# Graph attention on one NeuronCore: four heads' scores issued together, one product and one tanh per unit over four PSUM banks

## The chip, the cores and the metric

The kernel runs on one core of a Trainium2 chip. Its engines are TensorE (PE, and PEld for its weight loads), VectorE (DVE), ScalarE (ACT), GpSimd (POOL) and the queue of SyncE (SP), which only issues transfers here. The metric is the time of the program on the device in microseconds (us), as the median of the runs; lower is better.

## The reference

Sixteen graphs of 512 nodes with 256 features pass through four residual layers: a graph convolution, a mixture of 8 experts, a graph attention, and a mixture of 64 experts with a shared expert. The change lies in the third layer and in the pieces of the fourth that are computed alongside it:

```python
Xp = jnp.einsum('bnd,hdk->bhnk', X, Wp) + bp[None, :, None, :]
Xc = jnp.einsum('bhnk,hjk->bhnj', Xp, C)
attn = jnp.tanh(A[:, None] * jnp.einsum('bhnj,bhmj->bhnm', Xc, Xp))
Xh = jnp.einsum('bhnm,bhmk->bhnk', attn, Xp)
out = jnp.moveaxis(Xh, 1, 2).reshape(X.shape[0], X.shape[1], -1)
return jax.nn.relu(out)
# and of the fourth layer, for every token:
shared = jax.nn.silu(xf @ sw1) * (xf @ sw3) @ sw2
logits = xf @ gate_w.T          # scores, the best two experts, places in the experts' buffers
```

There are 8 heads of 32 features. X is the layer norm of the running activations x, and A is the weighted adjacency of each graph.

## The kernel before

The program is a chain of phases: the graph convolution, the first experts, the attention phase (`attention_phase`), and the second experts with the final sums. Every engine has its own program, written out by hand, and semaphores order them. There is no scheduler: an instruction waits behind all that stand ahead of it on its engine.

The attention phase loops over 16 graphs. The 8 heads of a graph form 2 groups of 4 (`HG = 4`), and the 512 nodes form 4 tiles of 128, so a graph has 8 units (`UNITS`), unit u being group u // 4 and tile u % 4. For each unit:

- `scores` (L1408, PE): for each of the 4 heads a product of 32 rows of weights with 512 columns, in three terms (high by high, high by low, low by high), into one PSUM bank per head of `p_s`. Head i lies on partitions 32i to 32i+31. The unit is done in two halves c, with two heads each, so a half has 6 matmuls.
- `products` (L1914, DVE): `att` = `p_s` times the adjacency, one instruction per half (128x1024 elements).
- `tanhs` (L1712, ACT): tanh in place on `att`, one instruction per half.
- `values` (L1421, PE): four heads' matmuls of `att` with 32 columns of weights each, accumulated over the 4 tiles of a group into `p_o`.

`att` has two buffers (`u % 2`), so the product of unit u waits for the values of unit u-2. `p_s` takes four of the eight PSUM banks, `p_o` one, and the three banks of `p_w` serve all side work. In the loop of PE a half's scores for unit u+1 are issued as soon as the product of the same half of unit u is done, while DVE multiplies the other half:

```python
for c in range(2):
    pe.wait_ge(prod_ready, 2 * (UNITS * b + u) + c + 1)
    ... scores(b, h, u + 1, c)        # in the last unit: the next graph's unit 0
    if c == 0:
        side_a(u)
        values(b, h, u - 1)
    else:
        side_b(u)
```

Side work is placed by hand after units. On PE: `turn` (L1428, transposes of the normalised x for the next graph and for the fourth layer), `turn_back` (L1434), `wide` (L1440, 512 columns by 256 features: two for the projection of the next graph, four for the shared expert of the graph before), `project_c` (L154 to L156), `logits` (L1452), `down` (L1459), `count_before` (L937, L939), and `keep_busy` (L1465), a matmul whose result nobody reads. The four shared `wide` and the two `down` exist only for the first 8 graphs (`OWN`); later graphs have `keep_busy` in their place and have their shared expert done in the next phase. I call graphs 2 to 8, which have all of it, full graphs, and graphs 10 to 15 late graphs. On ACT: `apply1` and `apply3` (layer norm applied, L1674 and L1683), the evacuations of `p_w`, `exps` (L1703), `silus` (L1707). On DVE: `stats1` and `stats3` (L175, L180), `add_attention` (L1824), `add_shared` (L1834), `split_projection` and `split_c` (L160), `gate_shared` (L1829), and the router's steps `scores_of`, `best_of`, `members_of`, `places_of`, `own_places_of`, `rows_of` (L1839 to L1907). On POOL: `weigh_moe0` and `add_moe0` (the first experts' results for the graph after next), `scale1` and `scale3`, and `scatter` of rows into the second experts' buffers. SP loads the adjacency of the next graph.

Of the kernel before, what the change touches and what calls it, by code (L numbers as in the profile page):

```python
# [23 lines left out]
P = 128  # L24
# [1137 lines left out]
def attention_phase(nc, a, m, sb):  # L1162
# [3 lines left out]
    with ExitStack() as ctx:  # L1166
# [54 lines left out]
        of = lambda f, par: 0 if f == 0 else 1 + par  # L1221

# [30 lines left out]
        def _(sp):  # L1253
# [22 lines left out]
            def graph(q, h, first, last):  # L1276
# [7 lines left out]
                if not last:  # L1284
                    if not is_at(b, 0):
                        sp.wait_ge(prod_ready, 2 * UNITS * b + T)
                    load_adj(b + 1, 1 - h)
# [9 lines left out]
        def _(pool):  # L1297
# [71 lines left out]
            def graph(q, h, first, last):  # L1369
                b = 2 * q + h  # L1370
                more = not (isinstance(b, int) and b + 2 >= B)
                if is_at(b, 0):
                    scale1(1)
                if more:
                    weigh_moe0(b + 2)
                if not is_at(b, 0):
                    scale3(b - 1)
                if more:
                    add_moe0(b + 2)
                if not (isinstance(b, int) and b < 2):  # L1380
                    scatter(q - 1, h, b - 2, 0)
                    scatter(q - 1, h, b - 2, 1)
                if more:
                    scale1(b + 2)

# [14 lines left out]
        def _(pe):  # L1400
            def scores(b, par, u, c):
# [3 lines left out]
                for n, (left, right) in enumerate(((xpth, xcth), (xpth, xctl), (xptl, xcth))):  # L1405
                    for i in (2 * c, 2 * c + 1):
# [4 lines left out]
            def values(b, par, u):  # L1411

                f, t = u // T, u % T
                pe.wait_ge(att_ready, 2 * (UNITS * b + u) + 2)
# [22 lines left out]
            def wide(w, f, src, bank, done, last_of=False):  # L1437

                for k in range(KD):
                    mm = pe.matmul(p_s[:, bank, :] if last_of else p_w[:, bank, :], w[:, k, f * P:(f + 1) * P], src[:, k, :],  # L1440
                                   start=(k == 0), stop=(k == KD - 1))
                mm.then_inc(done, 1)
# [24 lines left out]
            def project_first():  # L1467

                pe.wait_ge(xn_ready, 1)
                turn(xn, 0, 1, tr_done)  # L1470
                turn(xn, 1, 2, tr_done)
# [3 lines left out]
                wide(wp, 0, xt, 0, xpt_done)  # L1475
                wide(wp, 1, xt, 1, xpt_done)
                pe.wait_ge(xpt_ready, 1)
                turn_back(xpf[:, 0], 2, xp_done)
                pe.wait_ge(xp_ready, 1)
                pe.wait_ge(xpt_lo, 1)  # L1480
                pe.wait_ge(cd_split, 2)
                project_c(0, 0, 2)
                pe.wait_ge(xpt_ready, 2)
                pe.wait_ge(xpt_lo, 2)
                project_c(0, 1, 0)
                pe.wait_ge(xct_lo, 1)
                turn_back(xpf[:, 1], 2, xp_done)
                scores(0, 0, 0, 0)
                scores(0, 0, 0, 1)

            def graph(q, h, first, last):
# [4 lines left out]
                z, w = h, 1 - h  # L1496

                def side_a(u):
                    if u == 0 and late:
                        pe.wait_ge(member_ready, b - 1)  # L1500
# [4 lines left out]
                        count_before(pe, m, count, member, count_done)  # L1505
                    if u == 1 and post:
                        pe.wait_ge(ot_ready, GRP * b)
                        if late:
                            pe.wait_ge(r2_step, R2 * (b - 2) + 2)
                        else:  # L1510
                            pe.wait_ge(xp_ready, GRP * b + 2)
                        turn_back(ot[:, 1], 2, back_done)
                    if u == 2 and not last:
                        pe.wait_ge(xn_ready, b + 2)
                        if going_down:
                            pe.wait_ge(x4_ready, TB * (b - 2) + 1)
                        else:
                            pe.wait_ge(xct_lo, GRP * b + GRP)
                        turn(xn, 0, z, tr_done)
                        if post:  # L1520
                            pe.wait_ge(x3_ready, GRP * b)
                        else:
                            pe.wait_ge(xp_ready, GRP)
                        turn(xn, 1, 2, tr_done)
                    if u == 3 and post:
                        pe.wait_ge(xn3_ready, b)
                        if last:
                            pe.wait_ge(xct_lo, GRP * b + GRP)
                        turn(xn3[:, 1 - h], 0, z, tr3_done)
                        turn(xn3[:, 1 - h], 1, 2, tr3_done)  # L1530
                    if u == 4 and not last:
                        pe.wait_ge(xpt_ready, GRP * (b + 1) + 1)
                        if post:
                            pe.wait_ge(xt3_ready, KD * b)
                        turn_back(xpf[:, 0], 2, xp_done)
                    if u == 5:
                        pe.wait_ge(ot_ready, GRP * b + 1)
                        if not last:
                            pe.wait_ge(xpt_ready, GRP * (b + 1) + 2)
                        turn_back(ot[:, 0], z, back_done)  # L1540
                    if u == 6 and going_up:
                        pe.wait_ge(x3_ready, GRP * b + 1)
                        wide(ws3, 0, xt3, z, up_done)
                    if u == 7 and going_up:
                        pe.wait_ge(xp_ready, GRP * (b + 1) + 2)
                        wide(ws1, 1, xt3, 2, up_done)
                    if u == 6 and post and not going_up:
                        pe.wait_ge(x3_ready, GRP * b + 1)
                        keep_busy(z)
                    if u == 7 and post and not going_up:  # L1550
                        keep_busy(z)

                def side_b(u):
                    if u == 0 and going_down:
                        pe.wait_ge(hs_ready, KHS * (b - 1))
                        pe.wait_ge(xct_lo, GRP * b + GRP)
                        down(0, z)
                    if u == 1 and going_down:
                        down(1, w)
                    if u == 2 and not last:  # L1560
                        pe.wait_ge(xt_ready, KD * (b + 2))
                        if going_down:
                            pe.wait_ge(x4_ready, TB * (b - 1))
                        elif post:
                            pe.wait_ge(x3_ready, GRP * (b - 1) + 1)
                        else:
                            pe.wait_ge(xpt_ready, GRP)
                        wide(wp, 0, xt, w, xpt_done)
                    if u == 3 and not last:
                        if post:  # L1570
                            pe.wait_ge(xt3_ready, KD * (b - 1) + 1)
                        wide(wp, 1, xt, z, xpt_done)
                    if u == 4 and post:
                        pe.wait_ge(xt3_ready, KD * b)
                        if last:
                            pe.wait_ge(x3_ready, GRP * (b - 1) + 1)
                        logits(xt3, w)
                    if u == 4 and not last:
                        pe.wait_ge(xp_ready, GRP * (b + 1) + 1)
                        pe.wait_ge(xpt_lo, GRP * (b + 1) + 1)  # L1580
                        project_c(1 - h, 0, 2)
                    if u == 5 and going_up:
# [799 lines left out]
```

## Time and profile before

| | |
|---|---|
| median of 3 runs | 2228.31 us (2223.23 to 2232.1) |
| span of the profiled execution | 2229.1 us |
| PE busy over the span | 2052.3 us, 92% |
| DVE busy | 1538.2 us, 69% |
| ACT busy | 1246.9 us, 56% |
| POOL busy | 1062.8 us, 48% |
| attention phase, first to last product | 1024.5 to about 1741 us |

The profiled execution's own time is the span; it lies inside the range of the three runs. Busy shares are means over phases with different limits, so the attention phase has to be read by itself. The granted clock (PEclk) is the clock that TensorE was given: 1.00 stands for 2.4 GHz and 0.50 for 1.2 GHz.

### The profile page before, as it was taken

The page shows a single profiled execution, that of the slowest core. Times are in us where ns is not written, and L with a number is a line of the kernel's source. Part 1 is how long each engine was busy: PE and PEld are TensorE (multiplying, and loading weights), DVE is VectorE, ACT ScalarE, POOL GpSimd, SP SyncE. Part 2 cuts the span into 40 slices and gives each one's busy share as a digit, 9 for nine tenths or more (in the row PEclk, how much of TensorE's full clock was granted, in tenths as well). Part 3 has the DMA queues.
Part 4 walks back from the last instruction along what each step waited for, and adds up shares of the span by engine and source line. Part 5 has one row for each costly group of instructions (what it writes and reads, how often), then busy time and mean ns, then how long its engine had stood idle before and what let it go on. Part 6 is the DMA issues. An engine that isn't in the chain of part 4 may idle for free. (4 is left out here: it accounts for less than half of the span.)

```text
span 2229.1 us, 38475 instructions
## 1 busy us (share of the span) xinstructions
PE 2052.3 (92%) x12194; PEld 1499.7 (67%) x12194; DVE 1538.2 (69%) x3332; ACT 1246.9 (56%) x1870; POOL 1062.8 (48%) x1266
## 2 busy tenths in 40 slices
PE   7999999956999999967999999999999789999986
PEld 6988888845888888853454544444444478888853
DVE  6777777744666666654687778887876557767759
ACT  4444444414666666645766766675666257767630
POOL 3355555552333333326345565464642447777740
PEclk9999999977999999987999999998998899999998
DMA  7344445125555555643122211223221055556559
GB/s 288 146 170 172 171 171 181 39 82 172 167 184 175 176 183 172 179 152 132 57 95 83 98 62 62 77 82 103 74 67 32 6 181 182 187 167 191 187 204 350
DMA packets 138148, 315.42 MB, mean 142 GB/s; under 512 B 36990, under 2 KB 67808, under 8 KB 133952
## 3 DMA queue, kind: packets, MB, share of 16 engines
q1 hardware_dynamic: 106560, 271.77, 36.3%
q0 software_dynamic: 31488, 42.39, 5.5%
q8 instruction: 54, 0.88, 0.2%
q14 instruction: 46, 0.38, 0.1%
HBM read 206.67 MB, written 151.56 MB: 161 GB/s over the span
## 5 line engine op out<-in xcount | busy, mean ns | idle before, releaser
L1712 ACT ACTIVATE c_att<-c_att 128x1024 f32<-128x1024 f32 x256 | 270.0, 1057 | 210.5 <-DVE c_att L1914 208.3
L1914 DVE TENSOR_TENSOR c_att<-c_p_s,adj 128x1024 f32<-128x1024 f32 x256 | 301.1, 1216 | 86.5 <-PE c_p_o L1421 74.4
L2241 POOL DMA_INDIRECT moe_y<-d_y,d_goal x256 | 257.0, 1004 | 115.9 <-ACT d_y L2206 51.5
L995 POOL DMA_INDIRECT moe_y<-b_y,b_goal x144 | 155.4, 1079 | 327.8 <-DVE b_y L1047 293.9
L1408 PEld LDWEIGHTS c_p_s<-c_xcth,c_xpth 32*128 32x128 f32 x512 | 48.0, 185 | 208.3 <-issue 121.2
L154 PE MATMUL b_p_y<-b_w2h,b_hh 128*128 128x256 f32 x576 | 169.2, 294 | 7.4 <-DVE b_hl L160 4.0
L476 POOL DMA_INDIRECT moe_in<-a_xn,a_rows x128 | 141.5, 1106 | 57.6 <-issue 29.2
L160 DVE TENSOR_TENSOR b_hl<-b_ht,b_hh 128x512 fp32r<-128x512 f32 (+1 forms) x160 | 101.5, 638 | 88.8 <-ACT b_ht L1153 88.8
L155 PE MATMUL b_p_y<-b_w2l,b_hh 128*128 128x256 f32 x576 | 160.7, 279 | 0.0
L156 PE MATMUL b_p_y<-b_w2h,b_hl 128*128 128x256 f32 x576 | 160.6, 279 | 0.0
L1364 POOL DMA_INDIRECT moe_in<-c_xn,c_rows x128 | 130.6, 1020 | 53.8 <-issue 39.4
L1408 PE MATMUL c_p_s<-c_xcth,c_xpth 32*128 32x512 f32 x512 | 130.0, 505 | 27.0 <-DVE c_att L1914 26.2
L1421 PE MATMUL c_p_o<-c_att,c_xp 128*32 128x512 f32 x1024 | 143.4, 633 | 0.0
L160 DVE TENSOR_TENSOR d_xl<-d_p_tr,d_xh 128x1024 fp32r<-128x1024 f32 x64 | 78.4, 1225 | 75.7 <-ACT d_xh L2196 75.7
L154 PE MATMUL b_p_h<-b_xh,b_w1h 128*128 128x512 f32 (+1 forms) x320 | 120.7, 377 | 7.1 <-DVE b_w1l L160 4.7
L1330 POOL TENSOR_SCALAR c_nm<-c_mv 128x4 f32<-128x4 f32 x32 | 8.1, 254 | 245.4 <-DVE c_mv L180 245.2
L154 PEld LDWEIGHTS b_p_y<-b_w2h,b_hh 128*128 128x128 f32 x576 | 108.0, 188 | 18.5 <-DVE b_hl L160 15.9
L155 PE MATMUL b_p_h<-b_xl,b_w1h 128*128 128x512 f32 (+1 forms) x320 | 119.9, 375 | 0.0
L156 PE MATMUL b_p_h<-b_xh,b_w1l 128*128 128x512 f32 (+1 forms) x320 | 119.8, 374 | 0.0
L1148 ACT ACTIVATE b_w2h<-b_w 128x1024 fp32r<-128x1024 f32 x40 | 42.5, 1063 | 136.9 <-PE b_p_y L156 122.1
L1152 ACT ACTIVATE b_hh<-b_p_h,b_b 128x512 fp32r<-128x512 f32 (+1 forms) x160 | 103.8, 649 | 23.3 <-PE b_p_h L156 10.9
L1313 POOL TENSOR_SCALAR c_g<-c_g,c_ggate 128x256 f32<-128x256 f32 x120 | 110.8, 941 | 6.1 <-DMA c_g<-moe_y 3.1
(273 smaller groups left out, 6147.4 us busy)
## 6 DMA issues: line engine op xcount, KB each, us to landing
b_w<-in_moe_w SPq DMA_DIRECT2D x80, 512.0 KB, 4.3
moe_in<-b_zeros SPq DMA_DIRECT2D x65, 520.0 KB, 10.8
d_xin<-moe_in SPq DMA_DIRECT2D x64, 520.0 KB, 3.5
adj<-in_adj SPq DMA_DIRECT2D x32, 1024.0 KB, 5.6
b_xin<-moe_in SPq DMA_DIRECT2D x32, 520.0 KB, 5.9
c_g<-moe_y SPq DMA_DIRECT2D x32, 512.0 KB
moe_y<-c_zeros SPq DMA_DIRECT2D x32, 512.0 KB
d_w<-in_moe_w SPq DMA_DIRECT2D x64, 256.0 KB
```

Source lines behind the costliest of these rows:

```text
L154: pe.matmul(out, lh, rh, start=start, stop=False)
L155: pe.matmul(out, lh, rl, start=False, stop=False)
L156: return pe.matmul(out, ll, rh, start=False, stop=stop)
L160: return dve.tensor_tensor(low, whole, high.bitcast(F32), ALU.subtract)
L476: pool.indirect_dma_start(out=m["moe0_in"], out_offset=bass.IndirectOffsetOnAxis(ap=rows[:, h, k, t:t + 1], axis=0), in_=xn2[:, h, t, :], ...
L995: pool.indirect_dma_start(out=m["moe0_y"], out_offset=bass.IndirectOffsetOnAxis(ap=goal[:, h, t:t + 1], axis=0), in_=y[:, h, t, :], in_off ...
L1364: pool.indirect_dma_start(out=m["moe1_in"], out_offset=bass.IndirectOffsetOnAxis(ap=rows[:, par, k, t:t + 1], axis=0), in_=xn3[:, par, t, ...
L1408: mm = pe.matmul(p_s[:, i, :], left[r, s, tok], right[r, f, :], start=(n == 0), stop=(n == 2))
L1421: mm = pe.matmul(p_o[DH * i:DH * i + DH, :], xp[:, par, t, col:col + DH], att[:, u % 2, i, :], start=(t == 0), stop=(t == T - 1))
L1712: act.activation(part, part, ACT.Tanh).then_inc(att_ready, 1)
L1914: dve.tensor_tensor(att[:, u % 2, 2 * c:2 * c + 2, :], p_s[:, 2 * c:2 * c + 2, :], adj[:, h, u % T, :].unsqueeze(1).broadcast_to([P, 2, N] ...
L2241: pool.indirect_dma_start(out=m["moe1_y"], out_offset=bass.IndirectOffsetOnAxis(ap=goal[:, h, t:t + 1], axis=0), in_=y[:, h, t, :], in_off ...
```

## The change

Every unit is handled whole. `scores(par, u)` issues 12 matmuls, the four heads in turn within each of the three terms. One DVE instruction makes the product over all four banks (128x2048 elements) and one ACT instruction the tanh. PE now issues the scores of unit u at the head of iteration u, after the product of unit u-1, where it had issued those of unit u+1 after a half of the product of unit u. The banks of `p_w` get fixed names, and nearly all side work moves by a unit or so: the second `project_c` and the second `turn_back` of the projection go into units 0 and 1 of the graph that uses them, `logits` from unit 4 to 5, one shared `wide` into the next graph's unit 0, `apply1` from the first unit to the last of the graph before, and two `wide` are cut in two between neighbouring units. On POOL `add_moe0` comes before `scale3`, and `scale1` before the second `scatter`. The number of matmuls, of side instructions and of `keep_busy` per graph stays the same.

```diff
-            def scores(b, par, u, c):
+            def scores(par, u):
                 for n, (left, right) in enumerate(((xpth, xcth), (xpth, xctl), (xptl, xcth))):
-                    for i in (2 * c, 2 * c + 1):
+                    for i in range(HG):
                         mm = pe.matmul(p_s[:, i, :], left[r, s, tok], right[r, f, :], start=(n == 0), stop=(n == 2))
                 mm.then_inc(s_done, 1)
...
                 for u in range(UNITS):
-                    for c in range(2):
-                        pe.wait_ge(prod_ready, 2 * (UNITS * b + u) + c + 1)
-                        if u + 1 < UNITS:
-                            if u + 1 == T and c == 0:
-                                pe.wait_ge(xct_lo, GRP * b + 2)
-                            scores(b, h, u + 1, c)
-                        elif not last:
-                            scores(b + 1, 1 - h, 0, c)
-                        if c == 0:
-                            side_a(u)
-                            if u > 0:
-                                values(b, h, u - 1)
-                            elif post:
-                                values(b - 1, 1 - h, UNITS - 1)
-                        else:
-                            side_b(u)
+                    if post or u > 0:
+                        pe.wait_ge(prod_ready, UNITS * b + u)
+                    if u % T == 0:
+                        pe.wait_ge(xct_lo, GRP * b + u // T + 1)
+                    scores(h, u)
+                    side_a(u)
+                    if u > 0:
+                        values(b, h, u - 1)
+                    elif post:
+                        values(b - 1, 1 - h, UNITS - 1)
+                    side_b(u)
...
-            def tanhs(b, u, c):
-                act.wait_ge(prod_ready, 2 * (UNITS * b + u) + c + 1)
-                part = att[:, u % 2, 2 * c:2 * c + 2, :]
-                act.activation(part, part, ACT.Tanh).then_inc(att_ready, 1)
+            def tanhs(b, u):
+                act.wait_ge(prod_ready, UNITS * b + u + 1)
+                act.activation(att[:, u % 2], att[:, u % 2], ACT.Tanh).then_inc(att_ready, 1)
...
-            def products(b, h, u, c):
+            def products(b, h, u):
                 n = UNITS * b + u
-                if c == 0 and not (isinstance(n, int) and n < 2):
+                if n > 1:
                     dve.wait_ge(av_done, n - 1)
-                dve.wait_ge(s_done, 2 * n + c + 1)
-                dve.tensor_tensor(att[:, u % 2, 2 * c:2 * c + 2, :], p_s[:, 2 * c:2 * c + 2, :],
-                                  adj[:, h, u % T, :].unsqueeze(1).broadcast_to([P, 2, N]), ALU.mult)\
+                dve.wait_ge(s_done, n + 1)
+                dve.tensor_tensor(att[:, u % 2], p_s[:], adj[:, h, u % T, :].unsqueeze(1).broadcast_to([P, HG, N]),
+                                  ALU.mult)\
```

PE's side work by unit after the change (`side_b`, after the values, but for one piece of unit 4 that stands ahead of them as `side_a`), in a full graph: 0: `wide`, `count_before`, `project_c`; 1: `turn_back`, `down`, `turn_back`; 2: two `turn`, `down`; 3: one and a half `wide`; 4: half a `wide` (`side_a`), two `turn`; 5: two `turn_back`, `logits`; 6: `project_c`, one and a half `wide`; 7: one and a half `wide`. In a late graph the pieces of the shared expert fall away and `keep_busy` stands in units 0, 1, 6 and twice in 7.

DVE's side work after the product of the unit, in a full graph: 0: `gate_shared`, `places_of`; 1: `split_c`, `add_attention`, `stats3`, `add_shared`; 2: `own_places_of`, `add_shared`; 3: `rows_of`; 4: `split_projection`, `stats1`; 5: `add_attention`, `split_projection`; 6: `scores_of`, `best_of`; 7: `split_c`, `gate_shared`, `members_of`.

ACT's after the tanh: 0: `evac_c`; 1: `evac_tokens`; 2: two `evac_turned`, `apply3`; 3: `evac_projection`; 4: two `evac_turned`, `evac_projection`; 5: `exps`, `evac_tokens`; 6: `evac_c`, `silus`; 7: `silus`, `apply1`.

## Rows read from the trace of the kernel before

**Rows 1.** The page, its head.

```profile
span 2229.1 us, 38475 instructions
```

**Rows 2.** Windows: stretch, length, PE, PEld, DVE, ACT, POOL busy, PEclk, DMA, GB/s.

```profile
1024.00:1744.00 720.00, 691.54 (x3887) 324.36 (x3879) 549.08 (x1116) 468.08 (x637) 359.88 (x512) 0.96 0.23 77
...
1187.80:1234.60 46.80, 46.04 (x261) 22.55 (x259) 37.01 (x76) 31.66 (x44) 26.39 (x38) 1.00 0.26 86
...
1559.00:1601.20 42.20, 40.02 (x239) 18.39 (x237) 34.47 (x72) 27.74 (x40) 25.51 (x36) 1.00 0.29 92
```

**Rows 3.** Line 1703 on ACT, once per graph: first and last start in three stretches.

```profile
L1703 ACT ACT_TABLE_LOAD  x9: 1283/1283/1283, 1093.2 to 1467.3; - x9
...
L1703 ACT ACTIVATE c_sg<-c_p_w x2: 385/386/386, 1510.0 to 1558.6; 128x256 f32<-128x256 f32 x2
...
L1703 ACT ACTIVATE c_sg<-c_p_w x3: 384/385/386, 1558.6 to 1643.0; 128x256 f32<-128x256 f32 x3
```

**Rows 4.** Timeline of PE in a full graph: start, time, line, instructions, idle before.

```profile
1205.90 0.49 PE L1408 MATMUL c_p_s<-c_xcth,c_xpth 32*128 32x512 f32 x2
1206.24 0.39 PE L1408 MATMUL c_p_s<-c_xctl,c_xpth 32*128 32x512 f32 x2
1206.47 0.39 PE L1408 MATMUL c_p_s<-c_xcth,c_xptl 32*128 32x512 f32 x2
...
1207.31 1.07 PE L1421 MATMUL c_p_o<-c_att,c_xp 128*32 128x512 f32 x8
1208.31 0.50 PE L1408 MATMUL c_p_s<-c_xcth,c_xpth 32*128 32x512 f32 x2
...
1209.19 1.99 PE L1459 MATMUL c_p_w<-c_ws,c_sh 128*128 128x256 f32 x8
1211.12 0.50 PE L1408 MATMUL c_p_s<-c_xcth,c_xpth 32*128 32x512 f32 x2
...
1217.54 1.09 PE L1428 MATMUL c_p_w<-consts,c_xn 128*128 128x128 f32 x8
...
1232.14 2.00 PE L1452 MATMUL c_p_w<-c_wg,c_xt 128*128 128x64 f32 x16
...
1234.82 0.50 PE L1408 MATMUL c_p_s<-c_xcth,c_xpth 32*128 32x512 f32 x2
...
1238.21 1.98 PE L1440 MATMUL c_p_w<-c_xt,c_ws 128*128 128x512 f32 x4
1240.03 0.60 PE L1434 MATMUL c_p_w<-consts,c_xpf 128*128 128x128 f32 x4
1240.56 0.50 PE L1408 MATMUL c_p_s<-c_xcth,c_xpth 32*128 32x512 f32 x2
```

**Rows 5.** Timeline of PE in a late graph, same columns.

```profile
1564.51 0.50 PE L1408 MATMUL c_p_s<-c_xcth,c_xpth 32*128 32x512 f32 x2 [1.18 <-DVE c_att L1914]
...
1565.40 1.13 PE L1465 MATMUL c_p_w<-c_xt,consts 128*128 128x512 f32 x2
1566.45 1.07 PE L1421 MATMUL c_p_o<-c_att,c_xp 128*32 128x512 f32 x8
```

**Rows 6.** Timeline of DVE in a full graph, same columns.

```profile
1213.55 1.40 DVE L175 BATCH_NORM_STATS2 c_st<-x 128x6 f32<-128x256 f32 x4
...
1215.39 2.32 DVE L1914 TENSOR_TENSOR c_att<-c_p_s,adj 128x1024 f32<-128x1024 f32 x2
...
1218.23 0.16 DVE L1890 TENSOR_SCALAR c_fits<-c_ownpos 128x8 f32<-128x8 f32 x1
...
1221.79 2.34 DVE L1914 TENSOR_TENSOR c_att<-c_p_s,adj 128x1024 f32<-128x1024 f32 x2
```

**Rows 7.** Groups by line: busy us, mean ns of one, then idle before.

```profile
L1712 ACT ACTIVATE c_att<-c_att 128x1024 f32<-128x1024 f32 x256 | 270.0, 1057 | 210.5 <-DVE c_att L1914 208.3
...
L1693 ACT ACTIVATE c_xcth<-c_p_w 128x512 fp32r<-128x512 f32 x32 | 18.8, 587 | 3.9 <-PE c_p_w L156 3.9
```

**Rows 8.** Windows, columns as in rows 2, a stretch at the lower clock.

```profile
1516.00:1530.00 14.00, 13.93 (x43) 4.61 (x43) 7.39 (x22) 5.08 (x6) 11.31 (x15) 0.51 0.02 5
```

More of the change, by code:

```diff
@@ L1495, in graph, with side_b @@
                 going_up, going_down = post and b - 1 < OWN, late and b - 2 < OWN
[L1496 removed]
                 def side_a(u):
[L1499 to L1500 removed]
+                    if u == 4 and not last:
+                        wide(wp, 1, xt, LEFT, xpt_done, only=(1,))
+                def side_b(u):
+                    if u == 0:
+                        if going_down:
+                            wide(ws3, 1, xt3, RIGHT, up_done)
+                        elif late:
+                            keep_busy(RIGHT)
+                        if late:
+                            pe.wait_ge(member_ready, b - 1)
+                            if going_down:
+                                pe.wait_ge(hs_ready, KHS * (b - 2) + 1)
+                            else:
+                                pe.wait_ge(xp_ready, GRP * b + 1)
+                            count_before(pe, m, count, member, count_done)
+                        pe.wait_ge(xpt_ready, GRP * b + 2)
+                        pe.wait_ge(xpt_lo, GRP * b + 2)
@@ L1513, in side_a @@
-                    if u == 2 and not last:
-                        pe.wait_ge(xn_ready, b + 2)
+                        elif late:
+                            pe.wait_ge(sg_ready, b - 1)
+                        project_c(h, 1, LEFT)
+                    if u == 1:
+                        if post:
+                            pe.wait_ge(ot_ready, GRP * b)
+                            if late:
+                                pe.wait_ge(r2_step, R2 * (b - 2) + 2)
+                            else:
+                                pe.wait_ge(xp_ready, GRP * b + 1)
+                            turn_back(ot[:, 1], COUNT, back_done)
+                        if going_down:
+                            pe.wait_ge(hs_ready, KHS * (b - 2) + 2)
+                            down(0, RIGHT)
+                        elif late:
+                            keep_busy(RIGHT)
+                        pe.wait_ge(xct_lo, GRP * b + 2)
+                        turn_back(xpf[:, 1], LEFT, xp_done)
@@ L1544, in side_a @@
[L1544 to L1563, printed above, removed]
-                        elif post:
[L1565 to L1582, printed above, removed]
-                        pe.wait_ge(sg_ready, b)
-                        wide(ws1, 0, xt3, w, up_done)
-                    if u == 5 and not last:
-                        pe.wait_ge(xct_lo, GRP * (b + 1) + 1)
-                        turn_back(xpf[:, 1], 2, xp_done)
-                    if u == 6 and not last:
-                        pe.wait_ge(xpt_lo, GRP * (b + 1) + 2)
```

292 lines of the change are left out of this document (148 added, 144 removed).

## The prediction

> **What bounds the kernel now.** I read the page's head first, for the span, 2229.1 us [rows 1]; the median of the runs, 2228.3, is the same within their spread, so I sum against 2228. Then a window over the attention phase, which alone is touched: 720 us, PE busy 691.5, DVE 549.1, ACT 468.1 [rows 2]. Then one graph by itself. The step that happens once per graph comes every (1467.3 - 1093.2)/8 = 46.8 us in the graphs that carry the shared expert, and every (1643.0 - 1558.6)/2 = 42.2 us in late ones [rows 3]. In a full graph PE is busy 46.04 of 46.8 us, DVE 37.0, ACT 31.7; in a late one PE 40.0 of 42.2, DVE 34.5 [rows 2]. The reader is to see that PE is the bound: it idles 0.8 us in a full graph and 2.2 us in a late one, the latter in two pieces such as the 1.18 us wait for a product [rows 5].
>
> What is PE busy with? I read starts against starts, since matmul ends are modelled and overlap. A half of the scores is three rounds of two matmuls, starting at 0, 0.34 and 0.57 us, the round being 0.23 us; the values after it start 1.00 us before the next scores; those take 0.88 us until the next work starts [rows 4]. So a unit costs 2 x 0.88 (scores) + 1.00 (values) = 2.76 us, and a graph 22.1. The side work, likewise: `down` 1.93, a pair of `turn` 1.09 by its modelled end (I take 1.03), `logits` with `project_c` 2.68, `wide` 1.82 to 1.98 (I take 1.9), `turn_back` 0.53 to 0.6 [rows 4]; `count_before` lies between the end of a half's scores and the values, 1207.31 - 1205.90 - 0.88 = 0.5; `keep_busy` 1.05 [rows 5]. With 6 `wide`, 2 `down`, 2 pairs of `turn`, 4 `turn_back`, 2 `project_c` (0.88 each) and the rest this is about 23.8 us in a full graph. 22.1 + 23.8 + 0.8 idle = 46.7, against 46.8 found. In a late graph it is 17.5; 22.1 + 17.5 + 2.2 = 41.8 against 42.2.
>
> **The scores.** The two matmuls of a round read and fill different groups of 32 rows of the array and take 0.23 us together, what 512 columns take one after the other at 2.4 GHz (213 ns): they run side by side [rows 4]. The trace has no round of four. Bounds: four side by side cost what two do, a unit's scores falling from 1.76 to 0.88; or only two go at once, and nothing is saved. The values show four matmul groups of 32 columns side by side, 8 instructions in 1.00 us [rows 4], which is near the first bound, so I take it: 8 x 0.88 = 7.0 us of PE per graph.
>
> The Trainium skill has a rule against the full gain ("TensorE: Matmul & The Clock Gate", Measured speedup vs the span model): four row tiles of 32 at 512 columns gained 3.07 times, not 4. By it a round would be 4/3.07 x 0.23 = 0.30 us, an estimate, and 3 x 128 x 0.07 = 27 us of the gain would be lost, giving 2185. The pairs here show no such loss; no row here shows four.
>
> **What is lost with the halves.** Before, PE wrote one half while DVE read the other, so a product never waited for its scores. Now the chain of a unit is serial. From the start S of its scores: last result and hand-over at 1.04 (0.96 and 0.08); product 2.27 (a pair now takes 2.32 to 2.34 [rows 6], one instruction saves a start; bounds 2.2 and 2.35); tanh at S + 3.38, 2.0 long (1057 ns for 1024 elements and 587 for 512 [rows 7] extend to 1997; bounds 2.0 and 2.11); values at S + 5.44 at the earliest. Next scores can't start before S + 3.37. PE's own order would bring it to these values at S + 1.88 + s + 0.88, s being the side work of the unit. So values wait when s < 2.7, and the wait is longer when DVE reached the product late. Behind the waiting values stand all of `side_b` and the next scores.
>
> **A full graph by hand.** PE's side work after the change, by unit 0 to 7: 3.3, 3.1, 3.0, 2.85, 2.0, 3.0, 3.7, 2.85, all cost as above. DVE's: 1.25, 3.65, 2.0, 3.56 (`rows_of`, 1218.23 to 1221.79), 2.45, 1.2, 2.4, 2.95; `stats3` is 1.84 of it, 1213.55 to 1215.39 [rows 6]. After product 1 DVE has 3.65 us of side work, one us more than its gap, so product 2 is 1.0 late and its values hold PE 0.7. After product 3 `rows_of` makes product 4 start 1.8 after its scores; PE, whose unit 4 is short, waits 0.3 for it and 1.2 for its values. In unit 5 `logits` wait until ACT has evacuated the projection, some 0.1. Elsewhere the values are ready by under 0.3. ACT's heaviest spot, two evacuations and `apply3` after tanh 2, delays tanh 3 by 0.9 but PE comes later still. PE then needs 8 x 1.88 + 23.8 = 38.8 of work plus 2.3 of waits, 41.1 us. Gain 5.7.
>
> **A late graph by hand.** Side work of PE by unit: 2.4, 2.2, 1.0, 2.85, 2.0, 3.0, 1.9, 2.1, all but two below 2.7. Waits: 0.3 (values 0), 1.2 for product 2 and 1.2 for its values, 0.7 in unit 5, 0.2 before `logits`, 0.8 for values 6, 0.3 more spread. 15.0 + 17.5 + 4.7 = 37.2. Gain 5.0, cut to 4.9.
>
> **POOL and SP.** POOL is busy 26.4 of 46.8 us [rows 2] and would be 26 of 41. `rows_of` ends after some 22 us of the graph, so the two scatters and `scale1` end near 34; the next weighing and adding then end some 6 us into the next graph, and `scale3` waits for `stats3` at 12. Nothing late reaches ACT: `apply3` comes at 17. Moving `scale1` ahead of the second scatter serves `apply1` at the end of the graph; if it were late by all of a scatter (5 us), `turn` in unit 2 has 9 us left. The adjacency is loaded after two units, as before, 6 units ahead of use. Cost nothing.
>
> **Sum.** Graphs 2 to 8: 7 x 5.7 = 40. Graphs 1 and 9, with half of the shared work: 5 each, 10. Graphs 10 to 15: 6 x 4.9 = 29. Graph 0, with little side work, 3. Together 82.
>
> **The clock.** Over the phase the granted clock averages 0.96, which is 58 us at 1.2 GHz and 29 us of PE's time lost [rows 2]. One such stretch, 14 us at 0.51 [rows 8], lies in a late graph, the kind that has PE waits of over 1 us, and the once-per-graph step took 1558.6 - 1510.0 = 48.6 us across it instead of 42.2 [rows 3]: 6.4 more. I put half of the 29 us to the twelve waits of 1 us or more in the six late graphs (the split is an estimate): 1.2 us a wait. The change puts one such wait into each of nine graphs that had none and perhaps one more into the first: 10 x 1.2 = 12. Bounds: -29 (the low stretches vanish) and +74 (each graph gets one like that, 16 x 6.4, less the 29 there are). I take +12.
>
> 2228 - 82 + 12 = **2158**.
>
> **Rivals.** (a) *Four row groups don't run together.* PE saves nothing, while the serial chain puts some 1 us of waits for late products into each graph: 2228 + 16 + 12 = 2256, slower. For: no row shows four. Against: pairs at no cost, and values four wide. It decides from a round of 0.23 + 70/(3 x 128) = 0.41 us on. 0.06. (b) *The hand-over binds.* Each unit costs DVE its work plus the 1.04 of scores, which side work doesn't cover: 37.0 - 1.3 + 8.3 = 44.0 in a full graph, 34.5 - 1.3 + 8.3 = 41.5 in a late one; gains 9 x 2.8 + 6 x 0.7 = 29, with the clock's 12 a time of 2211. Against: side work stands just after the product, so while PE scores. A middle between this and my schedule is 2185. 0.16 for 2185 to 2215. (c) *The clock falls in every graph*: 2228 - 82 + 74 = 2220, no change; from 2 x 70 = 140 us more at 1.2 GHz on it is a loss. 0.09, a third each of slightly faster, same, slower. (d) *The waits don't come*: PE saves all, 16 x 7.0 = 112, less the clock's 0 to 12, 2115 to 2130. 0.12. My case: 0.57.
>
> **Numbers.** Mine alone spans 2130 to 2185: one us more or less of waits a graph is 16, a clock of -10 to +15 more. The range for 8 in 10 goes into (d) and (b): 2115 to 2206. Less than 0.5%, 11 us, can't be told from no change. Faster: 0.57 + 0.12 + 0.16 + 0.03 = 0.88; same 0.04 (c and the edge of b); slower 0.08 (a and the rest of c).
>
> **What would show it.** Rounds of x4 scores 0.23 us apart, the next work 0.88 us after their start; a once-per-graph step every 41 us, then every 37; PE busy near 39 of 41; PE waits of about 1 us for `att` from ACT in unit 5 and for the product in late graphs; product 2.2 to 2.3 us, tanh 2.0; DVE waiting for `c_p_s` where it hardly does now. It is wrong if rounds are 0.4 us, if the step still comes every 44 us with DVE never idle, or if PEclk over the phase falls below 0.90.

## The result, and the profile after

| | before | after |
|---|---|---|
| median of 4 runs each | 2230.2 us | 2128.5 us |
| span of the profiled execution | 2229.1 us | 2124.2 us |
| first to last product of the attention phase | 714.1 us | 607.5 us |

The ratio is 0.9545, 95% interval 0.9518 to 0.9572: 101.7 us less. Forecast were 70 us less, 2158, in a range of 2115 to 2206. All of it lies in the attention phase, which is 106.6 us shorter in the profiled executions. The phase is measured from the start of its first product on DVE to the start of its last.

First the windows of the changed kernel, over the phase and over one full graph; columns as in [rows 2].

```profile
1023.80:1631.30 607.50, 546.10 (x3865) 261.27 (x3868) 508.18 (x981) 444.54 (x508) 361.45 (x513) 0.99 0.28 91
...
1180.00:1219.90 39.90, 38.09 (x267) 18.97 (x259) 34.34 (x68) 30.25 (x36) 26.04 (x37) 1.00 0.28 96
```

In a full graph PE is still busy 38.1 us, but of 39.9 where it was 46.0 of 46.8 [rows 2]. The once-per-graph step on ACT, full graphs and then late ones, to be read against [rows 3]:

```profile
L1692 ACT ACT_TABLE_LOAD  x9: 1283/1283/1283, 1084.9 to 1404.1; - x9
...
L1692 ACT ACTIVATE c_sg<-c_p_w x4: 367/368/369, 1441.3 to 1553.5; 128x256 f32<-128x256 f32 x4
```

Full graphs take (1404.1 - 1084.9)/8 = 39.9 us instead of 46.8, late ones (1553.5 - 1441.3)/3 = 37.4 instead of 42.2.

The timeline of PE around the largest wait of a full graph, columns as in [rows 4]:

```profile
1188.90 0.50 PE L1409 MATMUL c_p_s<-c_xcth,c_xpth 32*128 32x512 f32 x4
1189.24 0.40 PE L1409 MATMUL c_p_s<-c_xctl,c_xpth 32*128 32x512 f32 x4
1189.47 0.40 PE L1409 MATMUL c_p_s<-c_xcth,c_xptl 32*128 32x512 f32 x4
1190.85 1.06 PE L1422 MATMUL c_p_o<-c_att,c_xp 128*32 128x512 f32 x8 [0.98 <-ACT c_att L1700]
```

The three rounds start at 0, 0.34 and 0.57 us, exactly as they did with two heads [rows 4], but now hold four. Then PE stands for 0.98 us until the tanh of the unit before is done. Over the whole phase the list of waits has these in place of the old ones (who waits, for whom: us in total, times, longest):

```profile
DVE c_att L1903 <- PE c_p_s L1409: 78.5, 60, 3.4
...
PE c_p_o L1422 <- ACT c_att L1700: 39.7, 56, 1.5
```

In the kernel before, the same view had DVE's products waiting for the values, and hardly ever for scores:

```profile
DVE c_att L1914 <- PE c_p_o L1421: 74.4, 70, 4.4
...
PE c_p_s L1408 <- DVE c_att L1914: 26.2, 30, 2.1
...
DVE c_att L1914 <- PE c_p_s L1408: 2.3, 5, 1.0
```

The product of 2048 elements takes 2.28 us and the tanh 1.91, means of 128 each (groups by line, columns as in [rows 7]):

```profile
L1903 DVE TENSOR_TENSOR c_att<-c_p_s,adj 128x2048 f32<-128x2048 f32 x128 | 292.1, 2282 | 82.4 <-PE c_p_s L1409 78.5
L1700 ACT ACTIVATE c_att<-c_att 128x2048 f32<-128x2048 f32 x128 | 244.6, 1911 | 148.1 <-DVE c_att L1903 148.0
```

### The profile page after: what moved, and what is told of

It reads as the page before. It is cut to its first block and busy times, and to the rows that moved or that the text cites. A ratio compares the mean times of both kernels' runs of the same rounds, so it can differ in the third digit from the quotient of the medians.

```text
span 2124.2 us, 38233 instructions
## 1 busy us (share of the span) xinstructions
PE 1911.5 (90%) x12194; PEld 1438.3 (68%) x12194; DVE 1500.9 (71%) x3204; ACT 1224.1 (58%) x1742; POOL 1066.3 (50%) x1266
## 5 line engine op out<-in xcount | busy, mean ns | idle before, releaser
L1903 DVE TENSOR_TENSOR c_att<-c_p_s,adj 128x2048 f32<-128x2048 f32 x128 | 292.1, 2282 | 82.4 <-PE c_p_s L1409 78.5
L1700 ACT ACTIVATE c_att<-c_att 128x2048 f32<-128x2048 f32 x128 | 244.6, 1911 | 148.1 <-DVE c_att L1903 148.0
L1422 PE MATMUL c_p_o<-c_att,c_xp 128*32 128x512 f32 x1024 | 137.7, 610 | 39.7 <-ACT c_att L1700 39.7
L155 PE MATMUL b_p_y<-b_w2l,b_hh 128*128 128x256 f32 x576 | 160.7, 279 | 0.0
L1365 POOL DMA_INDIRECT moe_in<-c_xn,c_rows x128 | 130.4, 1019 | 52.6 <-issue 38.1
L154 PE MATMUL b_p_h<-b_xh,b_w1h 128*128 128x512 f32 (+1 forms) x320 | 120.8, 377 | 6.3 <-DVE b_w1l L160 3.9
L155 PEld LDWEIGHTS b_p_y<-b_w2l,b_hh 128*128 128x128 f32 x576 | 108.3, 188 | 0.0
L156 PEld LDWEIGHTS b_p_y<-b_w2h,b_hl 128*128 128x128 f32 x576 | 108.0, 188 | 0.0
L154 PE MATMUL d_p_h<-d_xh,d_wh 128*128 128x512 f32 x256 | 106.9, 418 | 0.0
```

Source lines behind the costliest of these rows:

```text
L154: pe.matmul(out, lh, rh, start=start, stop=False)
L155: pe.matmul(out, lh, rl, start=False, stop=False)
L156: return pe.matmul(out, ll, rh, start=False, stop=stop)
L1365: pool.indirect_dma_start(out=m["moe1_in"], out_offset=bass.IndirectOffsetOnAxis(ap=rows[:, par, k, t:t + 1], axis=0), in_=xn3[:, par, t, ...
L1422: mm = pe.matmul(p_o[DH * i:DH * i + DH, :], xp[:, par, t, col:col + DH], att[:, u % 2, i, :], start=(t == 0), stop=(t == T - 1))
L1700: act.activation(att[:, u % 2], att[:, u % 2], ACT.Tanh).then_inc(att_ready, 1)
```

## The experiments

The first eight runs of the table were made on a chip on which the kernel before took 2335 to 2337 us. The changed kernel took about as long as on the other chip up to the end of the attention phase (its last product starts at 1639.3 instead of 1631.3 us), and from 1650 us to its end 587.9 instead of 474.2 us, in the last phase. So ratios to the kernel before on the same chip are compared, and the length of the attention phase, which is that of one trace per run.

| label | ratio to before (95%) | median, us | first to last product, us |
|---|---|---|---|
| after_again | 0.9574 (0.9519 to 0.9628) | 2238.7 | 613.2 |
| e1_pairs | 0.9630 (0.9578 to 0.9681) | 2243.0 | 615.3 |
| e2_pool_order | 0.9614 (0.9568 to 0.9660) | 2240.5 | 617.8 |
| e3_halves | 0.9544 (0.9501 to 0.9586) | 2223.9 | 600.7 |
| e4_stats_later | 0.9584 (0.9534 to 0.9634) | 2236.7 | 604.7 |
| e5_no_keep_busy | 0.9602 (0.9558 to 0.9645) | 2240.4 | 615.5 |
| e6_halves_stats | 0.9559 (0.9517 to 0.9602) | 2231.8 | 606.5 |
| e8_drained | 0.9976 (0.9944 to 1.0008) | 2334.1 | 710.7 |
| other chip: before_again | one run | 2227.5 | 704.0 |
| after_third | 0.9541 (0.9509 to 0.9572) | 2130.2 | 613.3 |
| e3_again | 0.9492 (0.9461 to 0.9523) | 2118.1 | 602.4 |
| e9_old_loop_whole | 1.0245 (1.0201 to 1.0290) | 2290.1 | 772.6 |

**e1_pairs: two heads after two heads, issued without a pause.**

```diff
-                for n, (left, right) in enumerate(((xpth, xcth), (xpth, xctl), (xptl, xcth))):
-                    for i in range(HG):
+                for c in range(2):
+                    for n, (left, right) in enumerate(((xpth, xcth), (xpth, xctl), (xptl, xcth))):
+                        for i in (2 * c, 2 * c + 1):
```

> The changed kernel with the 12 matmuls of a unit's scores issued as two groups of two heads (three rounds of two, twice), all else as changed. Theory (the gain is that four row groups run in one round): a unit's scores take 1.76 us of PE again instead of 0.88, in a stretch in which PE is the bound, so 128 x 0.88 = 113 us come back: 2235 to 2250, and the once-per-graph step 47 us in full graphs. Rival (the gain comes from the new places of the side work and from one instruction in place of two): at most 2160.

2243 us, beside 2239 for the changed kernel on this chip. The number lies inside the range of the theory only because this chip is slower: the once-per-graph step is 40.2 us and not 47. The ratio, 0.963, lies where the rival had it, but this says nothing for the rival's reason, as the trace shows. The one line of scores in e1_pairs, in a window of one burst (count, shortest/median/longest ns, first and last start):

```profile
L1410 PE MATMUL c_p_s<-c_xcth,c_xpth x4: 493/497/501, 1188.1 to 1188.1; 32*128 32x512 f32 x4
...
L1410 PE MATMUL c_p_s<-c_xctl,c_xpth x4: 388/392/393, 1188.4 to 1188.4; 32*128 32x512 f32 x4
...
L1410 PE MATMUL c_p_s<-c_xcth,c_xptl x4: 384/388/392, 1188.6 to 1188.7; 32*128 32x512 f32 x4
```

The second pair's first term, issued seventh, starts with the first pair's first term, and not after its third. The row groups took their work side by side in this order as in the other. So this kernel still had four at once, and told nothing of what that is worth.

**e8_drained: two heads, a wait until they are done, two heads.**

```diff
+                for c in range(2):
+                    for n, (left, right) in enumerate(...):
+                        for i in (2 * c, 2 * c + 1):
...
+                    if c == 0:
+                        mm.then_inc(s_done, 1)
+                        pe.wait_ge(s_done, 2 * (UNITS * b + u) + 1)
                 mm.then_inc(s_done, 1)
...
-                dve.wait_ge(s_done, n + 1)
+                dve.wait_ge(s_done, 2 * n + 2)
```

> The changed kernel with the scores of a unit as two groups of two heads, and PE waiting, between them, until the first group is done, so that four row groups never work at once. e1_pairs showed that the order of issue alone doesn't part them. Theory (the change gains because four row groups work at once): each unit costs PE 1.0 us more, where it is the bound, and lengthens the chain from product to product by as much: a step of 47 to 48 us in full graphs, 41 to 44 in late ones, 100 to 128 us more than the changed kernel, so no better than before. Rival: less than 60 us more, the rest of the gain lying in the placement.

2334 us, 95 more than the changed kernel beside it, and no better than the kernel before: ratio 0.9976. Its PE timeline, its step and its phase:

```profile
1179.62 0.50 PE L1410 MATMUL c_p_s<-c_xcth,c_xpth 32*128 32x512 f32 x2
1179.96 0.40 PE L1410 MATMUL c_p_s<-c_xctl,c_xpth 32*128 32x512 f32 x2
1180.19 0.40 PE L1410 MATMUL c_p_s<-c_xcth,c_xptl 32*128 32x512 f32 x2
1180.65 0.50 PE L1410 MATMUL c_p_s<-c_xcth,c_xpth 32*128 32x512 f32 x2
...
1181.55 1.06 PE L1426 MATMUL c_p_o<-c_att,c_xp 128*32 128x512 f32 x8
```

```profile
L1696 ACT ACT_TABLE_LOAD  x9: 1283/1283/1283, 1105.0 to 1472.2; - x9
```

```profile
1025.10:1735.80 710.70, 684.63 (x3865) 331.57 (x3869) 522.07 (x981) 446.30 (x508) 365.27 (x515) 0.95 0.24 78
```

The values start 1.93 us after the scores instead of 0.90, and a full graph takes (1472.2 - 1105.0)/8 = 45.9 us. That is 6.0 more, not 8 x 1.03 = 8.2: the waits for the tanh are gone, since PE comes later. Two things beside the row groups are in the 95 us. The wait itself puts 1.03 us between the two starts where the scores alone need 0.88, so 128 x 0.15 = 19 us are its own, if nothing hid them. And PEclk over the phase is 0.95 where the changed kernel on this chip has 0.99: the first two graphs, each some 10 us longer, and the last hold the low stretches. So without four row groups at once the new places and the single instructions, with such a wait in each unit, come out even with the kernel before; what they would be worth without the wait this run doesn't show. Full graphs at full clock carry the argument best: 45.9 us against 46.8 before and 39.9 after.

**e9_old_loop_whole: the kernel before, whole scores.** Does four at once suffice?

```diff
+                    pe.wait_ge(prod_ready, 2 * (UNITS * b + u) + 2)
                     for c in range(2):
-                        pe.wait_ge(prod_ready, 2 * (UNITS * b + u) + c + 1)
                         ... scores(b, h, u + 1, c) ...
-                        if c == 0:
-                            side_a(u)
-                            values(...)
-                        else:
-                            side_b(u)
+                    side_a(u)
+                    values(...)
+                    side_b(u)
```

> The kernel before with one edit: PE waits for both halves of the product and then issues all four heads' scores of the next unit; products and tanhs in halves, the side work and its places as before, and the values still one iteration behind. Theory (four row groups at once carry the gain, the new places little): full graphs fall from 46.8 to about 41 us a step. But here the values of unit u-1 come after the scores of u+1, and product u+1 waits for them, so a unit can't be shorter than 0.88 + 1.0 + 0.08 + 2.3 = 4.3 us and side_a: late graphs stay at 41. In all 50 to 60 us faster than the kernel before, 40 slower than the changed one. Rival (the places don't matter at all): within 15 us of the changed kernel.

2290 us, 59 slower than the kernel before. Neither expectation held. Its waits over the phase, its windows, and a stretch of PE:

```profile
PE c_p_s L1408 <- DVE c_att L1912: 160.7, 113, 3.4
DVE c_att L1912 <- PE c_p_o L1421: 120.8, 81, 4.7
```

```profile
1024.50:1797.10 772.60, 608.07 (x3854) 276.29 (x3854) 542.51 (x1108) 464.71 (x633) 358.95 (x512) 0.92 0.22 71
```

```profile
1226.38 2.00 PE L1459 MATMUL c_p_w<-c_ws,c_sh 128*128 128x256 f32 x8
1230.78 0.52 PE L1408 MATMUL c_p_s<-c_xcth,c_xpth 32*128 32x512 f32 x4 [2.40 <-DVE c_att L1912]
...
1231.71 1.65 PE L1428 MATMUL c_p_w<-consts,c_xn 128*128 128x128 f32 x8
1233.29 1.94 PE L1421 MATMUL c_p_o<-c_att,c_xp 128*32 128x512 f32 x8
```

The scores do run four wide. But the next product waits for the values of two units back, which stand behind its own scores and `side_a`; DVE's side work stands between products, and now PE waits for the whole product: 160.7 us against 26.2. I had priced the chain of a unit at 4.3 us and had not added DVE's side work, which can't run until the late product is done. PEclk is 0.92: of 772.6 us 0.08 is 62 us of PE's time, against 0.04 x 714 = 29 in the first trace of the kernel before and 0.02 x 704 = 14 in the second. How much of the slowdown is the clock's and how much the waits', this run doesn't part, since the waits let the clock fall and the low clock lengthens them. This kernel has the products and tanhs in halves, as e3_halves has, which is fast; so what it lacks is the loop with the values in the iteration of the next scores, and the side work placed for it. Those two weren't parted.

**e3_halves and e3_again: product and tanh in halves, scores whole.**

```diff
-                act.wait_ge(prod_ready, UNITS * b + u + 1)
-                act.activation(att[:, u % 2], att[:, u % 2], ACT.Tanh).then_inc(att_ready, 1)
+                for c in range(2):
+                    act.wait_ge(prod_ready, 2 * (UNITS * b + u) + c + 1)
+                    part = att[:, u % 2, 2 * c:2 * c + 2, :]
+                    act.activation(part, part, ACT.Tanh).then_inc(att_ready, 1)
...
+                for c in range(2):
+                    dve.tensor_tensor(att[:, u % 2, 2 * c:2 * c + 2, :], p_s[:, 2 * c:2 * c + 2, :],
+                                      adj[...].broadcast_to([P, 2, N]), ALU.mult).then_inc(prod_ready, 1)
```

> The changed kernel with product and tanh of a unit in two instructions of two banks each (the second tanh half starts after the second product half), scores still whole. Theory (PE waits for the tanh of the unit before, 39.7 us in the phase, because the whole tanh can't start until the whole product is done): tanh ends 0.85 us earlier after the product, the waits nearly go: 2100 to 2112. Rival (one instruction in place of two is part of the gain, 0.1 us on DVE and 0.15 us on ACT a unit on engines that bind): 2130 to 2145.

> e3_halves again, in five rounds beside the changed kernel. Theory: 10 to 15 us below the changed kernel in this call, the step of full graphs 39.3 against 39.9 us and of late ones 36.6 against 37.3. Rival (its lead was noise): within 5 us.

2223.9 us on the one chip and 2118.1 on the other, where the changed kernel beside it took 2130.2: 12 less, in every one of six runs below every one of the six (2116.0 to 2121.8 against 2125.3 to 2132.8). The theory's amount in the first expectation, 16 to 28, was too high; that of the second held, and so did its steps, 39.3 and 36.5 us. The waits of PE in e3_again:

```profile
PE c_p_s L1409 <- DVE c_att L1906: 17.4, 21, 2.7
...
PE c_p_o L1422 <- ACT c_att L1702: 10.7, 15, 1.1
PE c_p_s L1409 <- DVE c_xctl L160: 9.4, 7, 2.0
PE c_p_w L1435 <- DVE c_xctl L160: 7.0, 8, 2.3
```

The wait for the tanh falls from 37.2 us in after_third to 10.7; in its place 4.7 more for products and 9.2 more for `split_c` on DVE. One instruction in place of two, over the four banks, is a loss here. This is the fastest version found.

**e4_stats_later and e6_halves_stats.**

```diff
                         if post:
                             add_attention(b - 1, 1, COUNT)
-                            stats3(b - 1)
...
                     if u == 2:
+                        if post:
+                            stats3(b - 1)
```

> The changed kernel with stats3 moved on DVE from after product 1 to after product 2. Theory (side work of 3.6 us after product 1 makes product 2 late by 1.4 us, and PE waits 1 us for its values, in late graphs another 1.3 us for the product): product 2 starts with its scores, 1 us a full graph and up to 2 us a late graph less: 2105 to 2118. Rival (the layer norm then reaches ACT and PE late, or product 3 becomes late in its place): 2126 to 2140.

> Product and tanh in halves, as in e3_halves, and stats3 after product 2, as in e4_stats_later, in one kernel. Both take away PE's waits for the tanh, by different ends. Theory (they overlap only in units 2 and 3): full graphs 38.9 us a step, late ones 35.5, that is 10 us below e3_halves. Rival (e3_halves took all that was to be had in full graphs, and late graphs are bound by DVE): within 4 us of e3_halves.

The move shortens the phase by some 8 us (604.7 against 613.2), about 1 us in each full graph, as expected, and nothing in late graphs, where up to 2 were; the medians, 2236.7 and 2238.7, don't tell the two apart. With the halves it gains nothing over e3_halves: 606.5 against 600.7, 2231.8 against 2223.9. Full graphs take 39.3 us a step with the halves alone and with both, so in full graphs the wait was one, with two cures. Late graphs take 37.3 us with both and 36.5 with the halves alone: there the move brings a wait of its own. PE idles 22.0 us before its values in e6_halves_stats and 15.4 in e3_halves (whole traces). Neither amount expected of e6_halves_stats came: it is 8 us slower than e3_halves (3.5 us by the ratios), where the theory had 10 faster and the rival within 4. What the rival said of full graphs was right.

**e2_pool_order: GpSimd's order as before** (`scale3` ahead of `add_moe0`, `scale1` after both scatters).

> The changed kernel with GpSimd's order as before (weigh, scale3, add, both scatters, scale1). Theory (the short DVE instructions of rows_of were slow because GpSimd's adds ran beside them, and the new order took the adds elsewhere): they go back from 0.16 us to 0.35 to 0.45 on average, product 4 comes late, 0.5 to 1 us a graph: 2136 to 2145. Rival (the order of GpSimd is hidden): 2126 to 2132.

2240.5 us, the changed kernel on this chip being 2238.7, and full graphs take 40.0 us where it takes 40.2: the time doesn't tell them apart. `rows_of` had been the item: in the changed kernel it takes 1.4 us where it took 3.56 [rows 6]. In e2_pool_order, the same stretch of a full graph on DVE and on POOL:

```profile
1189.65 1.29 DVE L1871 TENSOR_TENSOR c_own<-c_oh,c_pos 128x256 f32<-128x256 f32 x2
...
1194.38 0.62 DVE L1879 TENSOR_SCALAR c_fits<-c_ownpos 128x8 f32<-128x8 f32 x1
...
1196.06 0.17 DVE L1896 COPY gate<-c_gk 128x8 f32<-128x8 f32 x1
...
1189.03 5.94 POOL L1326 TENSOR_TENSOR x<-x,c_g 128x256 f32<-128x256 f32 x8
```

The eight adds of `add_moe0` on POOL now run beside `own_places_of` and the first instruction of `rows_of`, and there DVE is slow; the copy comes after their end and is fast. All 14 graphs, groups by line, e2_pool_order and then the changed kernel:

```profile
L1871 DVE TENSOR_TENSOR c_own<-c_oh,c_pos 128x256 f32<-128x256 f32 x28 | 17.1, 652 | 0.0
...
L1879 DVE TENSOR_SCALAR c_fits<-c_ownpos 128x8 f32<-128x8 f32 x14 | 7.4, 532 | 0.0
...
L1871 DVE TENSOR_TENSOR c_own<-c_oh,c_pos 128x256 f32<-128x256 f32 x28 | 10.5, 417 | 0.0
...
L1879 DVE TENSOR_SCALAR c_fits<-c_ownpos 128x8 f32<-128x8 f32 x14 | 2.2, 161 | 0.0
```

In the kernel before the copy took 0.65 us in the 8 graphs in which it met the adds and 0.17 in the 6 in which it didn't. So the mechanism of the theory was right: several instructions of DVE are slow where they meet the adds, and the new order of GpSimd takes the adds away from them. The instructions of the two steps together take 3.15 us a graph in the changed kernel, 4.20 in e2_pool_order and 4.97 in the kernel before, so the order makes 1.05 of the 1.8 us and the rest goes with where in the graph they stand. Wrong was what it costs (8 to 17 us forecast): 1.05 us more of DVE's work a graph don't lengthen the full graphs.

**e5_no_keep_busy: without the filler matmuls.**

```diff
             def keep_busy(bank):
+                return
                 pe.matmul(p_w[:, bank, :], ident, xt3[:, 0, :], start=True, stop=True)
```

> The changed kernel without the 33 or so filler matmuls of keep_busy (their results are read by nobody). Theory (in late graphs PE is bound by waits for tanh, not by its work, and the fillers hold the clock): the step of late graphs falls from 37.3 to about 36 us, and PEclk falls, in all 2 to 20 us slower. Rival (the clock doesn't hang on them): 5 to 10 us faster.

2240.4 us against 2238.7: no difference that can be told, so neither expectation of the time held. The clock is another matter. PEclk over the phase is 0.96, where three traces of the changed kernel have 0.99, 0.99 and 0.98; below it two late graphs by themselves:

```profile
1020.70:1636.20 615.50, 534.97 (x3803) 255.15 (x3806) 511.97 (x982) 445.09 (x508) 363.60 (x516) 0.96 0.27 89
...
1450.60:1488.60 38.00, 30.38 (x227) 13.64 (x228) 32.19 (x67) 26.88 (x32) 25.74 (x37) 0.91 0.31 102
1488.60:1526.20 37.60, 29.55 (x227) 13.68 (x227) 32.07 (x65) 26.57 (x32) 25.52 (x37) 0.95 0.33 105
```

The full graphs, whose work holds no filler, stay at 1.00; each of the graphs 10 to 14 has 0.90 to 0.95, where in three traces of the changed kernel 13 of 15 such graphs have 1.00. All four executions agree: over the whole program the granted clock is 0.944 to 0.951 without the fillers and 0.954 to 0.960 with them, on the same chip. So the fillers do hold the clock in late graphs, and that half of the theory was right. The late step was to fall to 36 us and was 37.4 to 38.0. PE is busy 15 us less in the phase and loses 24 instead of 7 us to the clock (after_again), two amounts of the same size.

**before_again, after_again, after_third.**

> The kernel before, for a second trace of it. Theory (part of the gain that I forecast wrongly, the clock, is chance): its attention phase is again 700 to 720 us, with 46.8 us a step in full graphs, while the time at 1.2 GHz differs from the 51 us of the first trace by 15 us or more. Rival (the kernel before loses 50 us at 1.2 GHz as a rule): within 10 us of it.

> The changed kernel, unchanged, so that the variants have it beside them on one chip. The variants so far ran on a chip on which the kernel before took 2335 us, 105 more than where the change was first timed; the phase from first to last product was as long there, so the difference lies in the last phase. Theory: the change takes off about 100 us there too, ratio 0.955 to 0.960, and the once-per-graph step is 39.9 us in full graphs. Rival (part of the gain hung on the first chip): ratio above 0.965.

> The changed kernel in five rounds, for the comparison with e3_again and e9_old_loop_whole. Expected 0.955 to 0.960 of the kernel before, as in after_again.

The gain is the same on both chips: 98.6 and 100.8 us. The ratio of after_again, 0.9574, lies in the range expected, that of after_third, 0.9541, just below it. The clock of the kernel before is partly chance: its second trace has PEclk 0.98 over a phase of 704.0 us, the first 0.96 over 714.1. The time at 1.2 GHz was 34 us in the second and 51 in the first, so the theory of before_again held, though most full steps were 46.2 us and not 46.8:

```profile
1028.30:1732.30 704.00, 678.78 (x3854) 320.02 (x3854) 543.22 (x1108) 464.50 (x633) 361.18 (x512) 0.98 0.24 78
```

## Why the prediction was right, and what it had wrong

**What bounds the kernel** was right. PE was, with 98% of a full graph; taking 0.88 us of scores out of a unit took 6.9 us out of a full graph.

**Four row groups side by side** was the step on which all hung, chosen between bounds without a row. It was right at its favourable end: rounds 0.23 us apart with four, values 0.90 us after the scores' start. e8_drained shows the price of the term: 95 us when it is taken back, with a wait and a lower clock in them; 6.0 of the 6.9 us that a full graph gained. Rival (a) is out. By the Trainium skill's rule for four row tiles, a gain of 3.07 times ("TensorE: Matmul & The Clock Gate", Measured speedup vs the span model), the round would have been 0.30, an estimate; the trace doesn't show that loss between two and four.

**What is lost with the halves** was right in kind and nearly in size. PE waits for the tanh in the units that I named: 0.98 us for the values of unit 2 (forecast 0.7), then 0.6 for those of unit 4 (1.2). Together 1.6 us a full graph against 2.3. Full graphs came out at 39.9 instead of 41.1. The largest single cause is `rows_of`, taken at 3.56 us from one graph and found at 1.4: product 4 wasn't late. That graph was one of those in which GpSimd's adds ran beside it, and the change itself moves the adds; the prediction put the order of GpSimd at nothing on DVE. The rest is the tanh, 1.91 instead of 2.0, and 38.3 instead of 38.8 us of PE's work. Over eight steps that is 10 us of the 32 by which I was off. Late graphs were forecast at 37.3 and take 37.4; there the hand schedule was right to 0.1 us.

**The clock** was the step that failed: +12 us forecast, on the argument that each of nine graphs gets one more wait of a microsecond, at 1.2 us a wait. Full graphs got their waits, 0.98 and 0.6 us each, and lost nothing by them: over graphs 2 to 8 PEclk is 1.00 in both traces of the kernel before and in all three of the changed one. The stretch of eight full steps in the changed kernel:

```profile
1084.90:1404.10 319.20, 304.67 (x2079) 151.83 (x2076) 273.92 (x544) 242.52 (x281) 201.20 (x283) 1.00 0.26 86
```

The low stretches lie in the first two graphs and in late ones, and there the change took some away. Over the phase PEclk is 0.99, 0.99 and 0.98 where the kernel before has 0.96 and 0.98. At the means, (1 - 0.97) x 709 = 21 us of PE's time were lost before and (1 - 0.987) x 611 = 8 are lost now: 13 us gained instead of 12 lost, 25 of the 32. With the 10 of the full graphs this is a little more than 32, since the one is a mean over traces and the other isn't. The traces are few, but more executions say the same: on the chip of after_third the clock over the whole program is 0.959 in the mean of 11 executions of the kernel before and 0.965 in that of 6 of the changed one, some 16 us less lost.

Why late graphs fall less often stays open. PE waits longer there than before, 4.2 us a graph against 2.2, but waits of a microsecond or more are fewer: one in a late graph, where the kernel before has two. In these traces the clock goes with that number: graphs 2 to 8 of both kernels have none, and no fall; among graphs 10 to 14 the changed kernel has one in each, and a fall in 2 of 15; the kernel before has two, and a fall in 6 of 10; with three or more, without the fillers and in e9_old_loop_whole, every graph from 2 to 14 that has them shows a fall. That is an order seen in seven traces, not a tested cause. The forecast counted a new wait in each full graph, and not the one that went from each late graph.

**Rivals.** (b), the hand-over of 1.04 us in each unit, was right as a wait and wrong as a cost: DVE does wait 78.5 us for scores, but it isn't the bound. (c) didn't come. The time lies just outside my own case (2130 to 2185) and inside (d), 2115 to 2130, though by another way: the waits came, and the clock and the shorter `rows_of` made up for them. The sentence on POOL and SP, cost nothing, held for the time (e2_pool_order), not for DVE. One sum of chances is off by a hundredth: slower is (a) and a third of (c), 0.09 and not 0.08.

**What I had not seen** is that four at once isn't enough. e9_old_loop_whole has it and is 2.5% slower than the kernel before. In my sum the new place of the values stood only as a cost, a wait for the tanh. It is also what keeps products from waiting for values: DVE's 74.4 us of such waits are gone. In the kernel before they cost PE little, 26.2 us of waits for products; in e9_old_loop_whole they are 120.8 and PE's are 160.7.

## What to carry to other kernels

Matmuls on different row groups of 32 ran at once when they stood next to each other without a wait between, in either order tried; a hand-over in halves that puts a wait between them leaves the other half of the array idle. When a software pipeline loses a stage of overlap, write down the chain from each buffer's last reader to its next writer with all side work that stands on it: the same faster matmuls were worth -4.5% in one order of the loop and +2.5% in another. Merging two instructions into one saves a start and delays whatever could have begun on the first half; here the halves of product and tanh were worth 12 us. Before an instruction's time is taken from one graph, look at its spread over all graphs and at what runs beside it on the other engines. And when an experiment takes something out and the time stays, look at the single terms: without the fillers PE had 15 us less to do and lost 17 us more to the clock.

## What the runs showed of the hardware that was not expected

- Twelve matmuls of 32 rows, issued as two sets of six on different row groups, ran as three rounds of four, all four starting within 0.03 us of each other, as when issued four by four: the start of the seventh did not wait for the sixth.
- Several DVE instructions took up to four times as long where they ran beside adds of 128x256 on GpSimd: 0.59 us instead of 0.16 (a scalar operation on 128x8, e2_pool_order), 0.65 instead of 0.17 (a copy of 128x8, kernel before), 0.94 instead of 0.42 (a product of 128x256, kernel before). Others took the same beside them and alone, such as a reduction (0.69) and a reciprocal (0.18).
- The granted clock stayed at 1.00 through full graphs in which PE waited 0.98 and 0.6 us, and fell in each of the graphs 10 to 14 once some 31 filler matmuls were gone.
- A product over four PSUM banks took 2.28 us and one over two banks 1.22; a tanh of 2048 elements 1.91 us and one of 1024 1.06.
- One chip needed 588 us, the other 474, from 1650 us to the end of the same program, with the phases before nearly alike.
